# Shared expert's gate and up spread between the steps of the last batch's routing, its rows finished around the plan, and turnings late in the first round of expert tiles

## The chip, the cores and the metric

The kernel runs on one core of a Trainium2 chip. The metric is device time in microseconds (us) of one execution. Five engines run their own instruction streams and meet at semaphores: PE (TensorE, matmuls and transposes), DVE (VectorE), ACT (ScalarE), POOL (GpSimd, here almost only indirect DMAs) and SP (SyncE, plain DMAs).

## The reference, cut to what matters

One transformer layer in float32 on 4 batches of 512 tokens with 512 features: a modulated layer norm, linear attention, a second modulated layer norm, and a mixture of 64 experts with the best 8 per token, plus a shared expert that every token passes through.

```python
h = _layernorm(x) * (1 + cb) + sb                       # rows "h2"
logits = h @ gate_w.T                                   # 64 experts
topv, topi = top_k(logits, 8); rw = softmax(topv)
inter = silu(gate) * up                                 # per expert, 512 -> 128
out = einsum(inter * W[:, :, None], dp_w)               # 128 -> 512
sh_inter = silu(x @ sh_gate_w.T) * (x @ sh_up_w.T)      # shared expert
out = out + sigmoid(x @ sh_gate1_w.T) * (sh_inter @ sh_down_w.T)
x = x + gb * out
```

## The kernel before, in words

Everything is one unrolled program but for the loop over the experts' tiles. Attention and routing go batch by batch; `LAST` is batch 3. The order on each engine is the order in which the code is written, and each engine waits only at semaphores (`s_...`).

**Routing of the last batch** goes in two halves of two 128-token tiles each. For a half, PE turns the normalized rows (`turn_h2_half`), ACT copies them out of PSUM (`turned_h2_half`), PE scores them against the gate weights (`score_half`), DVE picks the best 8 (`choose_half`), PE ranks each pick within its expert (`rank`, two small bf16 matmuls per tile), and DVE works out the picks' slots (`places_half`). POOL writes each pick's token number to its slot in DRAM (`slot_table`) by an indirect DMA of 128 numbers (L587, 32 per batch). In the code, `landed` makes POOL wait after every 8 of them until they have landed.

**The plan** follows: PE counts each expert's tokens (`s_cnt`), DVE makes tiles of them (`s_ntile`), PE sums them up (`s_cum`), DVE compares (`s_past`), PE spreads that out (`s_flat`), DVE writes `plan` (`s_plan`, 2). Before the counting, DVE finishes the last batch's rows (`finish_h2`: 4 tiles, a multiplication and an addition each) and makes the routing weights (`weights`, ends with `s_wt`).

**SP** stores the finished rows when `s_h2` is complete and the routing weights when `s_wt` is; only behind these two in its order stand the loads of the first experts' weights (`load_w`) and of the slot table's parts (`load_table`), which alternate: weights 1, part 0, weights 2 and 3, part 1, and so on.

**Shared expert.** Batch 0's is done early. `KEPT` (batch 1), `HELD` (2) and `LAST` (3) come after the routing: `shared_gate_up` is 8 matmuls of 128x512 (4 for the gate, 4 for the up half; each shows as two rows of PE in the trace), ACT makes the silu (`shared_silu`), DVE the product (`shared_inter`), PE the product with the down weights (`shared_down`), DVE adds it to x (`shared_sum`). Between them stand DVE's first token lists (`first_tokens`: numbers 0 to 2 need part 0 of the table, 3 and 4 part 1), which release POOL's first gathers of rows (L634).

**The experts' tiles** go in rounds of 8, 20 rounds. Per tile of 128 tokens: PE turns the gathered rows (`turn`, L1710), gate and up (L1715), turning of the product (L1730), down (L1723); ACT and DVE work between. Round 0 is written out, the others loop. In the step of tile t, PE turns tile t+2 before the gate and up of tile t. ACT's order in a step is: copy of turned tile t+2 (`take_x`), weights of tile t (`own_pairs`), silu of tile t.

## Time and profile before

| | |
|---|---|
| median of 3 runs | 1062.57 us (1063.09, 1053.07, 1062.57) |
| profiled execution | 1062.77 us, span 1060.9 us |
| busy share of the span | PE 88%, PEld 54%, DVE 52%, ACT 25%, POOL 46% |
| mean granted TensorE clock | 0.956 of full |
| chain that ended last | PE 60%, "another core or an unknown queue" 10%, DVE 9%, issue 6%, DMA 5% |

The span runs from the first to the last instruction; 1.9 us of the execution lie outside it. The stretch that the change touches runs from about 304 us (last batch's rows turned) to about 410 us (end of round 0).

### The profile page before, as it was taken

The page shows a single profiled execution, that of the slowest core. Times are in us where ns is not written, and L with a number is a line of the kernel's source. Part 1 is how long each engine was busy: PE and PEld are TensorE (multiplying, and loading weights), DVE is VectorE, ACT ScalarE, POOL GpSimd, SP SyncE. Part 2 cuts the span into 40 slices and gives each one's busy share as a digit, 9 for nine tenths or more (in the row PEclk, how much of TensorE's full clock was granted, in tenths as well). Part 3 has the DMA queues.
Part 4 walks back from the last instruction along what each step waited for, and adds up shares of the span by engine and source line. Part 5 has one row for each costly group of instructions (what it writes and reads, how often), then busy time and mean ns, then how long its engine had stood idle before and what let it go on. Part 6 is the DMA issues. An engine that isn't in the chain of part 4 may idle for free.

```text
span 1060.9 us, 18619 instructions
## 1 busy us (share of the span) xinstructions
PE 929.2 (88%) x3569; PEld 570.0 (54%) x3570; DVE 546.4 (52%) x1457; ACT 261.8 (25%) x789; POOL 491.5 (46%) x480
## 2 busy tenths in 40 slices
PE   6999999999875789888989999888998899887697
PEld 2344444445342356666666666666666666655243
DVE  4777767885854333333433334333434334333888
ACT  2133132123120023322322223223332233222000
POOL 0500254264557355555555555555555555555500
PEclk9999999999987889999999999999999999999699
DMA  9940030030032326666656666666667665796697
GB/s 345 333 142 1 1 95 8 34 95 1 1 104 76 117 62 204 218 200 195 215 183 224 234 225 201 212 198 210 210 206 245 207 202 173 260 393 250 228 420 316
DMA packets 68519, 192.07 MB, mean 181 GB/s; under 512 B 19926, under 2 KB 20438, under 8 KB 68104
## 3 DMA queue, kind: packets, MB, share of 16 engines
q1 hardware_dynamic: 38232, 120.28, 32.3%
q0 software_dynamic: 30256, 71.43, 20.5%
q8 instruction: 12, 0.20, 0.1%
q14 instruction: 19, 0.16, 0.1%
HBM read 158.98 MB, written 52.54 MB: 199 GB/s over the span
## 4 chain that ended last, share of the span: by engine, by line
PE 60%; another core or an unknown queue 10%; DVE 9%; issue 6%; DMA 5%; DVEq 1%; ACTq 1%; ACT 1%; POOLq 0%; SPq 0%; POOL 0%
PE bank L1715 18%; PE bank L1723 12%; PE bank L1483 7%; PE bank L1710 6%; PE bank L1530 5%; PE bank L1784 3%; PE bank L1494 2%; PE bank L1730 2%; PE bank L1596 2%; DMA wqkv<-y_rows 1%; PE bank L1615 1%; DMA front<-y_rows 1%; DVE front L1328 1%; DMA y_rows<-front,sid 1%
## 5 line engine op out<-in xcount | busy, mean ns | idle before, releaser
L1715 PE MATMUL bank<-wqkv,h2T 128*128 x1280 | 313.2, 388 | 0.5 <-issue 0.5
L644 POOL DMA_INDIRECT y_rows<-front,sid x160 | 163.6, 1023 | 216.8 <-issue 82.4
L1715 PEld LDWEIGHTS bank<-wqkv,h2T 128*128 128x128 f32 x1280 | 238.1, 197 | 28.9 <-issue 1.6
L587 POOL DMA_INDIRECT slot_table<-pair,place x128 | 129.1, 1009 | 181.1 <-DVE place L1050 118.6
L634 POOL DMA_INDIRECT front<-h_rows,gid x167 | 170.9, 1023 | 74.4 <-issue 46.5
L1342 DVE COPY front<-bank 128x128 f32<-128x128 f32 x160 | 46.6, 291 | 271.8 <-remote 156.5
L1723 PE MATMUL bank<-wqkv,front 128*128 x320 | 173.7, 625 | 0.8 <-DVE front L1342 0.8
L830 ACT ACTIVATE h2T<-bank 128x512 f32<-128x512 f32 x162 | 96.5, 596 | 253.9 <-PE bank L1710 144.5
L1710 PEld LDWEIGHTS bank<-const,front 128*128 128x128 f32 x648 | 83.2, 146 | 100.4 <-issue 96.6
L1336 DVE COPY front<-bank 128x512 f32<-128x512 f32 x160 | 110.0, 688 | 45.1 <-PE bank L1723 34.1
L1483 PE MATMUL bank<-wqkv,front 128*128 128x512 f32 x256 | 113.8, 595 | 0.0
L1710 PE MATMUL bank<-const,front 128*128 128x128 f32 x648 | 102.5, 283 | 10.2 <-issue 5.5
L1730 PE MATMUL bank<-const,front 128*128 128x128 f32 x160 | 46.3, 290 | 58.7 <-DVE front L1328 55.3
L1483 PEld LDWEIGHTS bank<-wqkv,front 128*128 128x128 f32 x256 | 47.5, 190 | 56.3 <-issue 54.9
L1328 DVE SCALAR_TENSOR_TENSOR front<-bank,wgt,front 128x128 f32<-128x128 f32 x160 | 56.0, 350 | 29.9 <-ACT front L836 24.9
L836 ACT ACTIVATE front<-bank 128x128 f32<-128x128 f32 x160 | 43.4, 271 | 105.9 <-PE bank L1715 67.5
L1730 PEld LDWEIGHTS bank<-const,front 128*128 128x128 f32 x160 | 22.6, 141 | 78.6 <-DVE front L1328 57.8
L1494 PE MATMUL bank<-front,wqkv 128*128 128x512 f32 x128 | 59.3, 607 | 0.0
L1530 PE MATMUL bank<-front 128*128 128x512 f32 x128 | 56.6, 594 | 2.5 <-DVE front L1040 2.4
L1723 PEld LDWEIGHTS bank<-wqkv,front 128*128 128x128 f32 x320 | 49.1, 194 | 14.2 <-issue 3.4
L1784 PE MATMUL bank<-front,const 128*128 128x512 f32 x92 | 44.6, 635 | 8.5 <-DMA front<-y_rows 8.5
L845 ACT ACTIVATE wgt<-front 128x1 f32 x160 | 32.5, 203 | 72.4 <-issue 46.8
(254 smaller groups left out, 769.9 us busy)
## 6 DMA issues: line engine op xcount, KB each, us to landing
wqkv<-in_experts SPq DMA_DIRECT2D x64, 768.0 KB
front<-y_rows SPq DMA_DIRECT2D x20, 768.0 KB, 9.9
wqkv<-y_rows SPq DMA_DIRECT2D x12, 768.0 KB, 11.6
front<-in_w_mod SPq DMA_DIRECT2D x5, 1024.0 KB, 10.3
x<-in_x SPq DMA_DIRECT2D x4, 1024.0 KB, 11.1
h_rows<-h SPq DMA_DIRECT2D x4, 1024.0 KB
out_dram<-x SPq DMA_DIRECT2D x16, 256.0 KB, 8.4
wqkv<-in_w_in SPq DMA_DIRECT2D x3, 1024.0 KB, 13.5
```

The lines of the kernel that those rows point to most:

```text
L587: pool.indirect_dma_start(out=slots[:, :], out_offset=bass.IndirectOffsetOnAxis(ap=place[b % 2][:, i, k:k + 1], axis=0), in_=pair[:, b * T ...
L634: pool.indirect_dma_start(out=xg[s], out_offset=None, in_=h2_rows[:, :], in_offset=bass.IndirectOffsetOnAxis(ap=gid[:, s:s + 1], axis=0), ...
L644: pool.indirect_dma_start(out=y_rows[:, :], out_offset=bass.IndirectOffsetOnAxis(ap=sid[:, s:s + 1], axis=0), in_=yb[s % YBUFS], in_offset ...
L830: sc.activation(h2T[:, s % 4, :], bank[s % 2][:, :], ACT.Copy).then_inc(s_xT, 1)
L1336: ve.tensor_copy(yb[s % YBUFS], bank[4 + s % 2][:, :]).then_inc(s_y, 1)
L1483: mm = pe.matmul(bank[2 + j][:, :], hT[:, k, i * P:(i + 1) * P], win[:, k, (j + 1) * D:(j + 2) * D], start=(k == 0), stop=(k == KC - 1))
L1494: mm = pe.matmul(bank[4 + c % 2][:, :], win[:, k, c * P:(c + 1) * P], hT[:, k, :], start=(k == 0), stop=(k == KC - 1))
L1530: mm = pe.matmul(bank[4 + i % 2][:, :], qT[:, k, i * P:(i + 1) * P], woa[:, k, :], start=(k == 0), stop=(k == KC - 1))
L1710: mm = pe.transpose(bank[s % 2][:, k * P:(k + 1) * P], xg[s][:, k * P:(k + 1) * P], ident)
L1715: mm = pe.matmul(bank[2 + s % 2][:, 0:GU], xT[s % 4][:, k, :], wqkv[:, bass.ds(w + k * GU, GU)], start=(k == 0), stop=(k == KC - 1))
L1723: pe.matmul(bank[4 + s % 2][:, :], iT[s % 2], wqkv[:, bass.ds(w + KC * GU, D)], start=True, stop=True).then_inc(s_d, 1)
L1730: pe.transpose(bank[6 + s % 2][:, 0:P], inter[s % 2], ident).then_inc(s_I, 1)
```

## The change

Six edits, in three groups.

1. On PE, the gate and up of the shared expert, before a block behind the routing, are cut into pieces of 4 or 2 matmuls that stand between the steps of the last batch's routing (KEPT all, HELD's gate half) and of the plan (HELD's up half, LAST's both).
2. On DVE, `finish_h2` and `weights` of the last batch leave their place ahead of the counting. Two tiles are finished behind `s_ntile`, two behind `s_past`; `weights` stands behind the plan.
3. On POOL, `landed` is not called for batch 2. On PE, in round 0, the turning of tile t+2 stands behind tile t's gate and up, tile t-1's turning and tile t-2's down.

```diff
@@ POOL
                     scatter(b, n, n + TOPK)
-                    landed(b, n + TOPK)
+                    if b < LAST - 1:
+                        landed(b, n + TOPK)
@@ DVE, last batch
                         places_half(b, j, td)
-                    finish_h2(ve, b)
-                    weights(b)
                     ve.wait_ge(s_cnt, 1)
...
                     ve.tensor_copy(tiles_f[:, :], tiles_f[:, :]).then_inc(s_ntile, 1)
+                    finish_h2(ve, b, range(0, HT))
                     ve.wait_ge(s_cum, 1)
...
                     ve.tensor_scalar(past[:, :], const[0:EV, C_FLAT:C_FLAT + PLAN], cum[:, 0:1], None, ALU.is_ge).then_inc(s_past, 1)
+                    finish_h2(ve, b, range(HT, TPB))
                     shared_inner(KEPT)
...
                     ve.tensor_copy(plan[:, 1, :], plan_f[:, 1, :]).then_inc(s_plan, 1)
+                    weights(b)
                     ve.wait_ge(s_plan, 2)
                     first_tokens(range(0, 3))
@@ PE, shared_gate_up
-            def shared_gate_up(b, halves=range(2)):
+            def shared_gate_up(b, halves=range(2), chunks=range(KC)):
...
-                    for k in range(KC):
+                    for k in chunks:
...
-                if j == 1:
+                if j == 1 and k == KC - 1:
                     mm.then_inc(s_shg, 1)
@@ PE, last batch
                     turn_h2_half(b, 0)
+                    shared_gate_up(KEPT, range(0, 1))
                     score_half(b, 0)
+                    shared_gate_up(KEPT, range(1, 2), range(0, KC // 2))
                     turn_h2_half(b, 1)
                     rank(b, range(0, HT))
+                    shared_gate_up(KEPT, range(1, 2), range(KC // 2, KC))
                     score_half(b, 1)
+                    shared_gate_up(HELD, range(0, 1))
                     rank(b, range(HT, TPB))
@@ PE, plan
-            shared_gate_up(KEPT)
             pe.wait_ge(s_rd, BATCH)
             pe.matmul(bank[6][0:EV, 0:1], ...).then_inc(s_cnt, 1)
-            shared_gate_up(HELD, range(0, 1))
+            shared_gate_up(HELD, range(1, 2))
             pe.wait_ge(s_ntile, 1)
...
-            shared_gate_up(HELD, range(1, 2))
+            shared_gate_up(LAST, range(0, 1))
             pe.wait_ge(s_past, 1)
...
+            shared_gate_up(LAST, range(1, 2))
             shared_down(KEPT)
-            shared_gate_up(LAST)
             shared_down(HELD)
             shared_down(LAST)
@@ PE, a step of a round
-                    turn(t + 2, r + (s + 2) // ROUND, (s + 2) % ROUND)
+                    if again:
+                        turn(t + 2, r + (s + 2) // ROUND, (s + 2) % ROUND)
...
                         down(t - 2, (s - 2) % 2, w[s - 2])
+                    if not again:
+                        turn(t + 2, r + (s + 2) // ROUND, (s + 2) % ROUND)
```

In PE's order, from the second scoring of the last batch to the count, stood before (bank7 is the scoring, bank6 the rank and the count, bank2 and bank3 KEPT's gate and up):

```order
L1578 MATMUL bank7<-gate_w,xn 128x65 [waits s_arow,s_top,s_h2T]
L1578 MATMUL bank7<-gate_w,xn 128x65 x7
L1626 MATMUL bank6<-mask,tri_bf 128x65 [waits s_mask,s_rd,s_woa]
L1627 MATMUL bank6<-seen,ones_bf 128x65
L1626 MATMUL bank6<-mask,tri_bf 128x65 [waits s_mask]
L1627 MATMUL bank6<-seen,ones_bf 128x65
L1596 MATMUL bank2<-front,shared_w 128x512 [waits s_kvr,s_sht,s_again,s_shw]
L1596 MATMUL bank2<-front,shared_w 128x512 x3
L1596 MATMUL bank3<-front,shared_w 128x512 x4
L1689 MATMUL bank6<-ones_bf,seen 65x1 [waits s_rd]
```

and stands now, from the last piece of KEPT ahead of that scoring (bank4 is HELD's gate half):

```order
L1598 MATMUL bank3<-front,shared_w 128x512 [waits s_kvr,s_sht,s_again,s_shw]
L1598 MATMUL bank3<-front,shared_w 128x512
L1580 MATMUL bank7<-gate_w,xn 128x65 [waits s_arow,s_top,s_h2T]
L1580 MATMUL bank7<-gate_w,xn 128x65 x7
L1598 MATMUL bank4<-h2T,shared_w 128x512 [waits s_kvr,s_or,s_shw]
L1598 MATMUL bank4<-h2T,shared_w 128x512 x3
L1628 MATMUL bank6<-mask,tri_bf 128x65 [waits s_mask,s_rd,s_woa]
L1629 MATMUL bank6<-seen,ones_bf 128x65
L1628 MATMUL bank6<-mask,tri_bf 128x65 [waits s_mask]
L1629 MATMUL bank6<-seen,ones_bf 128x65
L1694 MATMUL bank6<-ones_bf,seen 65x1 [waits s_rd]
```

The count stood behind KEPT's 8 matmuls and stands now right behind the rank; HELD's gate half moved ahead of the rank.

In DVE's order, behind the last batch's places (`place1`), stood before:

```order
L1050 TENSOR_TENSOR place1<-spot_c,spot_p 128x16 [waits s_vd]
L391 TENSOR_TENSOR h2<-h2,rows_b 128x512 [waits s_tpC,s_rows_b]
L393 TENSOR_TENSOR h2<-h2,rows_b 128x512 [waits s_h2m]
...
L1080 SCALAR_TENSOR_TENSOR wtok,esum<-etop,mask 128x64 [waits s_ww,s_ex]
L1080 SCALAR_TENSOR_TENSOR wtok,esum<-etop,mask 128x64 x3
L1082 TENSOR_SCALAR sh1<-esh 128x4
L1083 RECIPROCAL gate_sh<-sh1 128x4 [waits s_vw]
L1084 RECIPROCAL rsum<-esum 128x4
L1085 TENSOR_TENSOR wtok<-wtok,rsum 128x256 [waits s_vw]
L1289 CAST count_i<-bank6 65x1 [waits s_cnt]
```

and between the plan and the first token stands now:

```order
L1311 CAST plan<-plan_f 1x200 [waits s_v]
L1312 CAST plan<-plan_f 1x200
L1081 SCALAR_TENSOR_TENSOR wtok,esum<-etop,mask 128x64 [waits s_ww,s_ex]
L1081 SCALAR_TENSOR_TENSOR wtok,esum<-etop,mask 128x64 x3
L1083 TENSOR_SCALAR sh1<-esh 128x4
L1084 RECIPROCAL gate_sh<-sh1 128x4 [waits s_vw]
L1085 RECIPROCAL rsum<-esum 128x4
L1086 TENSOR_TENSOR wtok<-wtok,rsum 128x256 [waits s_vw]
L1212 TENSOR_LOAD plan [waits s_tbl0,s_plan]
```

The weights, on which SP's store and with it all loads of the table wait, stood ahead of the count and stand now between the plan and the first token, which itself waits for part 0 of the table.

## Rows read from the trace of the kernel before

**Rows 1.** Stretches: length, then PE, PEld, DVE, ACT, POOL busy; clock, DMA share, GB/s

```profile
304.00:331.00 27.00, 11.66 (x60) 9.21 (x59) 11.83 (x56) 7.25 (x16) 18.30 (x20) 0.59 0.03 3
...
340.00:352.00 12.00, 1.70 (x6) 0.64 (x4) 1.26 (x9) 0.60 (x1) 7.15 (x8) 0.76 0.62 179
...
410.00:985.00 575.00, 511.01 (x2285) 366.94 (x2283) 216.56 (x612) 169.29 (x609) 314.56 (x309) 0.97 0.65 220
```

**Rows 2.** PE in order of time: start, us, line, tile, count [idle before <-releaser]

```profile
306.54 2.00 PE L1578 MATMUL bank<-gate_w,xn 128*128 128x65 f32 x16 [1.65 <-ACT xn L769]
...
316.85 3.68 PE L1578 MATMUL bank<-gate_w,xn 128*128 128x65 f32 x16 [1.44 <-issue]
...
328.90 8.98 PE L1596 MATMUL bank<-front,shared_w 128*128 128x512 f32 x16
...
337.75 3.68 PE L1596 MATMUL bank<-h2T,shared_w 128*128 128x512 f32 x8
...
352.34 5.79 PE L1596 MATMUL bank<-h2T,shared_w 128*128 128x512 f32 x8
...
362.37 7.03 PE L1596 MATMUL bank<-xn,shared_w 128*128 128x512 f32 x16
...
376.10 1.04 PE L1710 MATMUL bank<-const,front 128*128 128x128 f32 x8
...
379.46 1.95 PE L1715 MATMUL bank<-wqkv,h2T 128*128 x8
```

**Rows 3.** DVE in order of time, from a scoring's copy to the first token

```profile
312.90 0.29 DVE L1130 COPY logit<-bank 128x130 f32<-128x130 f32 x1 [3.20 <-remote]
...
326.48 0.29 DVE L1130 COPY logit<-bank 128x130 f32<-128x130 f32 x1 [6.49 <-remote]
...
331.11 0.69 DVE L391 TENSOR_TENSOR h<-h,rows_b 128x512 f32<-128x512 f32 x1
...
339.46 0.48 DVE L1085 TENSOR_TENSOR wtok<-wtok,rsum 128x256 f32<-128x256 f32 x1 [1.17 <-DVE rsum L1084]
350.12 0.15 DVE L1289 CAST count_i<-bank 65x1 int32<-65x1 f32 x1 [10.18 <-issue]
...
360.06 0.24 DVE L1311 CAST plan<-plan_f 1x200 int32<-1x200 f32 x1
361.34 0.15 DVE L1214 TENSOR_SCALAR gid<-tbl 128x1 int32 x1 [1.03 <-issue]
```

**Rows 4.** ACT in order of time, the silu of the kept batch

```profile
347.99 0.60 ACT L789 ACTIVATE shared_act<-bank 128x512 f32<-128x512 f32 x1 [16.32 <-remote]
```

**Rows 5.** POOL in order of time, scatters (L587) and gathers (L634)

```profile
300.61 0.96 POOL L587 DMA_INDIRECT slot_table<-pair,place  x1 [5.36 <-DMA slot_table<-pair,place]
...
331.47 1.16 POOL L587 DMA_INDIRECT slot_table<-pair,place  x1 [1.06 <-issue]
...
348.32 0.96 POOL L587 DMA_INDIRECT slot_table<-pair,place  x1 [0.30 <-remote]
362.49 1.04 POOL L634 DMA_INDIRECT front<-h_rows,gid  x1 [13.21 <-DVE gid L1214]
...
390.42 1.04 POOL L634 DMA_INDIRECT front<-h_rows,gid  x1 [6.30 <-DVE gid L1214]
```

**Rows 6.** SP in order of time, loads of the table's parts 0 and 1

```profile
341.20 0.34 SPq L488 DMA_DIRECT2D tbl<-slot_table  x1
...
350.47 0.33 SPq L488 DMA_DIRECT2D tbl<-slot_table  x1
```

**Rows 7.** DMA issues from 340 to 352 us, KB and us to landing

```profile
tbl<-slot_table SPq DMA_DIRECT2D x1, 16.0 KB, 3.9
```

**Rows 8.** PE in order of time, tile 7 of round 0 and the loop

```profile
407.74 1.89 PE L1715 MATMUL bank<-wqkv,h2T 128*128 x8
...
439.23 1.46 PE L1715 MATMUL bank<-wqkv,h2T 128*128 x6
```

**Rows 9.** DVE in order of time, in the loop

```profile
442.57 0.29 DVE L1342 COPY front<-bank 128x128 f32<-128x128 f32 x1 [5.62 <-remote]
```

## The prediction

> **What bounds the kernel now.** I read the page first, then the table of stretches, then each engine in order of time from 300 to 410 us. The loop of the experts' tiles, 410 to 985 us, is PE's: busy 511 of 575 us at a clock of 0.97 [rows 1]. The change leaves it and the end as they are, so what counts is when the loop gets going. Ahead of it, from 304 to 331 us, no engine is full: PE 11.7 of 27 us, at a mean clock of 0.59 [rows 1]. There the chain goes PE, ACT, PE, DVE and back, twice, for the routing, then through the plan. It ends in two things: the first gather, at 362.5 us [rows 5], and PE's first turning, at 376.1 us [rows 2], behind all of the shared expert. The first gather waited 13.2 us for DVE's token numbers, POOL having been free since 349.3 us [rows 5]; they followed the plan, done at 360.3 us [rows 3].
>
> One thing in this chain is no work. PE's rows end well before those who need them start. The second scoring is over at 320.5 us, DVE copies it at 326.48 [rows 2, 3]; KEPT's gate and up is over before HELD's begins at 337.75, ACT's silu of it starts at 347.99 [rows 2, 4]; DVE, ready at 339.94 us, gets the count only at 350.12 [rows 3]. I call this late results. It comes in the loop too: DVE idle 5.6 us until 442.57 while PE's rows go on [rows 8, 9]. I have no row that names the cause, and most of the uncertainty below is about what becomes of it.
>
> **The change, part by part.**
>
> *Count.* Before, DVE's places ended at 331.1 us, then came 8.8 us of finishing and weights (331.11 to 339.94), then 10.2 us of waiting [rows 3]. Now the count stands directly behind rank on PE and behind the places on DVE. Neither the 8.8 us nor KEPT's 8 matmuls (16 rows, 6.9 us at full clock, from 0.43 us a row) stand ahead of it. The wait of 10.2 us fell where DMA was busy for 0.62 of the time; from 304 to 331 us, where the count now goes, it was 0.03 [rows 1]. Bounds: 10.2 us of lateness again, or none. I take none, since a count this early meets neither that traffic nor that queue of gate and up. Count at 331.6 rather than 350.1: 18.5 us earlier.
>
> *Gate and up between the routing steps.* A piece of 4 matmuls is 3.4 us at full clock and double at half. The one ahead of the first scoring pushes it from 306.5 to 308.3, its end to 310.3; DVE used the result only at 312.90 [rows 2, 3], so lateness covers this; without that cover it costs 1.8 us. The next (2 matmuls, 1.7 us) lies beside ACT's norm. The one ahead of the second scoring could cost 1.7 us; against that the second scoring took 3.68 us where the first took 2.00 for the same 16 rows [rows 2], the clock having fallen to 1.2 GHz while PE idled; with PE fed it should take 2.0. These two cancel. HELD's gate half stands ahead of the last rank, but DVE has 2.2 us of choosing in between, and lateness ahead of that. Bounds for the whole: +5 (no cover) to -4. I take -1.3, giving a count at 330.3.
>
> *Count to plan.* Before: 350.12 to 360.3, 10.2 us, of which 5.8 us is a piece of HELD at mostly half clock [rows 2, 3]. Now this stretch has, on DVE in order: the count's steps 1.6, the sum 0.7, two tiles finished 2.7 (8 operations at 0.69 make four tiles 5.3 [rows 3]), the comparison 1.2, then PE's LAST piece and the spreading, 0.5 to 3, in whose shadow lie the other two tiles 2.7, the product 0.7 and the plan's own 1.4. Sum about 10.8. Plan at 341, 19 us earlier.
>
> *Weights and table.* This edit gives back. `weights` takes 3.5 us (the rest of the 8.8 after 5.3), so `s_wt` comes at 344.6: later than before (339.94) by 4.7 us. Queued behind it on SP: the store, then part 0 of the table, issued 1.3 us after the weights were done (341.20) and landing 3.9 us later [rows 3, 6, 7], then weights of experts 2 and 3, then part 1, issued 10.5 us after them (350.47) [rows 6]. Before, part 0 had landed long before the plan; now DVE waits for it: 344.6 + 5.2 = 349.8, first gather about 351. POOL is free by then, since it was at 349.3 with its last 14 scatters following places at 331.1 [rows 5], which now come 1.3 us earlier. First gather 11.5 us earlier.
>
> *POOL without waits for batch 2.* The longest of them was 5.4 us, at 300.6 [rows 5]. POOL then reaches the last batch's scatters earlier, but those wait for the places. Before, the second half's started right with its places, at 331.47 [rows 5], so the queue was no bound. Worth 0 in the likeliest case; if places come early (below), it lets the scatters follow.
>
> *PE's end of the shared expert.* Before, LAST's gate and up ran 362.4 to 369.2 and the down products to 376.1 [rows 2]. The 6.9 us are now done earlier, but what is late next is DVE: HELD's product stands behind tokens 0 to 2 (part 0), LAST's behind tokens 3 and 4 (part 1). Part 1 lands at 344.6 + 10.5 + 3.9 = 359; then the product 0.7, the down products 3.4 at full clock or up to 6.9 at half (PE has idled). First turning at about 365.5 instead of 376.1: 10.6 us earlier.
>
> *Round 0.* From first turning to tile 7's gate and up PE took 31.6 us (376.1 to 407.74 [rows 2, 8]) for 8 tiles; the loop needs 575 us for the other 152, 3.8 each with its own late results, 3.4 in busy time [rows 1]: 27 to 30 us. Waiting for gathers made part of the difference: gather 5 went out at 390.42, after POOL had waited 6.3 us for DVE [rows 5]. Turning late lets PE do gate and up of tile t while t+2 is still on its way. Its cost: `take_x` of t+2 stands ahead of tile t's silu on ACT, so that silu now follows the late turning instead of running in the shadow of gate and up; at most the 0.5 us of a turning a tile (two took 1.04 [rows 2]), 4 us in all. Bounds -5 to +4; I take -3, as the waits for gathers weigh more.
>
> **Sum:** -10.6 - 3 = -13.6 on the profiled execution's 1062.8 us, which is 0.2 over the median: **1049 us**. The fast one of the three runs before (1053.07) shows that some 10 us come and go by themselves.
>
> **Rivals.**
>
> *The late results go away.* Those of this stretch fall where PE mostly waits (11.7 of 27 us busy [rows 1]), and feeding it is what the pieces do. Then places come some 12 us earlier (4.4 ahead of the first copy, 6.0 ahead of the second [rows 2, 3], less at the rank). The scatters then bind: 20 of them at 1.26 us from about 316.8 end at 342. Plan 333, weights 336.5, part 0 at 341.7, first gather 343, part 1 at 351, first turning 357.5: 18.6 + 3 earlier, **1041**. Against: in the loop PE is fed and they occur [rows 8, 9].
>
> *The wait moves with the count.* If the 10.2 us of lateness meet the count wherever it is, the plan comes at 351, `s_wt` at 355, part 1 at 369, first turning at 376: only round 0 is left, **1060**. For it: DVE got both scoring results late as well, with no DMA traffic about.
>
> *The late results are PE's real pace.* KEPT's 16 rows then took 328.9 to 347.99, 1.2 us a row [rows 2, 4], not the 0.43 of the records. Now 24 such rows stand between the first turning of the last batch's rows and the count, against 16 before: 9.5 us later, and LAST's piece before the plan adds 3.7. Plan at 371 to 373, weights 3.5, part 1 at 390, first turning at 395 against 376.1; less round 0's 3: +16, **1079**. Between the likeliest case's -13.6 at 0.43 us a row and this +16 at 1.2 the break-even lies near 0.8. Against: the records do slow down with the granted clock (8.98 us for KEPT's 16 rows, 7.03 for LAST's, [rows 2]), so they follow the array. [...]
>
> **How the numbers follow.** Likeliest case 0.44, results on time 0.23, wait moved 0.24, real pace 0.09. What a measurement can tell from no change is about 1%, 10.6 us: faster means under 1052, slower over 1073. Faster: nearly all of the first (0.38) and second (0.22), 0.60. Slower: the last, 0.09. The rest 0.31. The range leaves out the last case and the tails of the others below 1036 and above 1063, together under 0.2.
>
> **What the profile of the changed kernel would show.** DVE's count within 2 us of the places' end (if 10 us later: wait moved). KEPT's pieces in PE's rows between 305 and 315, clock full there. SP's load of part 0 about 1.3 us behind DVE's weights, and DVE idle between them and the first token, which shows the new wait; first gather near 351; first turning near 365; in round 0 PE's gate and up with no gather ahead of them. The prediction is wrong if places move by more than 3 us either way, or if tile 7's gate and up is not some 13 us ahead of 407.7.

## The result and the profile after

The kernel after takes 1078.62 us (median of 4 runs, 1077.78 to 1079.36), the kernel before 1062.36 us beside it: a ratio of 1.0154, 95% interval 1.0111 to 1.0196. It is slower by 16 us, where 1049 us was forecast. All ratios here and below leave out single executions far above the rest of their kernel (three in all, of 1059.1, 1069.2 and 2416.1 us). The profiled execution took 1079.36 us, span 1077.5 us; PE was busy 87% at a clock of 0.953.

The stretches of [rows 1] after the change (same columns):

```profile
304.00:331.00 27.00, 16.74 (x50) 8.04 (x48) 11.89 (x41) 4.11 (x7) 7.68 (x8) 0.81 0.01 0
340.00:352.00 12.00, 9.59 (x31) 4.08 (x30) 7.43 (x31) 3.64 (x8) 8.95 (x11) 0.98 0.02 1
410.00:985.00 575.00, 513.63 (x2305) 368.77 (x2304) 217.45 (x618) 171.08 (x616) 315.69 (x309) 0.97 0.66 222
```

The loop is as it was. From 304 to 325 us PE is not at the routing at all, but still at the projection ahead of it, in code that the change does not touch. POOL of the kernel after, in order of time (its row of batch 2's 32 scatters begins and ends with the first two lines, the row of the last batch's 20 with the next two; then gathers 0 and 5):

```profile
272.77 0.96 POOL L587 DMA_INDIRECT slot_table<-pair,place  x1 [19.00 <-DVE place L1051]
...
313.01 0.96 POOL L587 DMA_INDIRECT slot_table<-pair,place  x1 [0.30 <-issue]
336.50 0.96 POOL L587 DMA_INDIRECT slot_table<-pair,place  x1 [22.53 <-DVE place L1051]
...
360.71 0.96 POOL L587 DMA_INDIRECT slot_table<-pair,place  x1 [0.30 <-issue]
375.39 1.04 POOL L635 DMA_INDIRECT front<-h_rows,gid  x1 [13.72 <-DVE gid L1215]
...
403.11 1.05 POOL L635 DMA_INDIRECT front<-h_rows,gid  x1 [6.08 <-DVE gid L1215]
```

DVE of the kernel after in order of time, which answers to [rows 3]: the additions of the last projection (L1099), the two scoring copies, the count, the sum, the plan, the end of the weights, tokens 0 and 3:

```profile
306.38 0.69 DVE L1099 TENSOR_TENSOR x<-bank,x 128x512 f32<-128x512 f32 x1 [13.49 <-issue]
...
318.31 0.69 DVE L1099 TENSOR_TENSOR x<-bank,x 128x512 f32<-128x512 f32 x1 [9.39 <-remote]
...
331.48 0.29 DVE L1131 COPY logit<-bank 128x130 f32<-128x130 f32 x1 [0.47 <-PE bank L1580]
...
337.71 0.29 DVE L1131 COPY logit<-bank 128x130 f32<-128x130 f32 x1 [1.49 <-PE bank L1580]
...
343.38 0.15 DVE L1288 CAST count_i<-bank 65x1 int32<-65x1 f32 x1
...
350.13 0.15 DVE L1299 COPY cum<-bank 65x1 f32<-65x1 f32 x1 [2.52 <-issue]
...
364.93 0.35 DVE L1308 TENSOR_TENSOR plan_f<-bank,const 1x200 f32<-1x200 f32 x1 [10.37 <-remote]
...
367.27 0.42 DVE L1086 TENSOR_TENSOR wtok<-wtok,rsum 128x256 f32<-128x256 f32 x1
374.24 0.15 DVE L1215 TENSOR_SCALAR gid<-tbl 128x1 int32 x1 [6.54 <-issue]
...
384.38 0.15 DVE L1215 TENSOR_SCALAR gid<-tbl 128x1 int32 x1 [4.89 <-issue]
```

PE of the kernel after: the turning of the last batch's rows, the product for the plan, the first turning and tile 0's gate and up, tile 7's:

```profile
325.17 1.04 PE L1569 MATMUL bank<-const,h 128*128 128x128 f32 x8
...
351.85 0.88 PE L1703 MATMUL bank<-past,ones 65*1 65x200 f32 x2
...
391.02 1.04 PE L1715 MATMUL bank<-const,front 128*128 128x128 f32 x8
392.55 1.99 PE L1720 MATMUL bank<-wqkv,h2T 128*128 x8 [0.49 <-issue]
...
427.25 3.27 PE L1720 MATMUL bank<-wqkv,h2T 128*128 x8
```

Read together: DVE waits 13.5 and 9.4 us for the projection's results (0.8 and 0.9 us before the change) while POOL issues scatters without a break, and the turning of the last rows comes at 325 instead of about 304 us. The first turning is 14.9 us later than before (376.10 in [rows 2]); most of the loss is there. Between, all went much as designed: no late copies, the count right behind the places, at a clock of 0.98. Then POOL's next row begins at 336.5, and the plan's numbers, whose PE rows end at 352.7, reach DVE at 364.9. That is 3 us behind the end of POOL's row; the addition at 318.31 came 4 us behind the end of the row ahead of it.

### The profile page after: what moved, and what is told of

It is laid out like the page before. It is cut to its first block, busy times and chain, and to the rows that moved or that the text cites. A ratio compares the mean times of both kernels' runs of the same rounds, so it can differ in the third digit from the quotient of the medians.

```text
span 1077.5 us, 18621 instructions
## 1 busy us (share of the span) xinstructions
PE 932.7 (87%) x3569; PEld 568.0 (53%) x3570; DVE 546.0 (51%) x1457; ACT 261.8 (24%) x789; POOL 490.6 (46%) x480
## 4 chain that ended last, share of the span: by engine, by line
PE 62%; another core or an unknown queue 10%; DVE 8%; issue 7%; DMA 3%; ACTq 1%; DVEq 1%; ACT 1%; SPq 0%; POOLq 0%
PE bank L1720 20%; PE bank L1728 12%; PE bank L1485 7%; PE bank L1715 6%; PE bank L1532 4%; PE bank L1792 4%; PE bank L1735 2%; PE bank L1496 2%; DMA front<-y_rows 2%; PE bank L1598 1%; DVE front L1330 1%; PE bank L1558 1%; DVEq L1212 1%; ACTq L841 1%
## 5 line engine op out<-in xcount | busy, mean ns | idle before, releaser
L587 POOL DMA_INDIRECT slot_table<-pair,place x128 | 128.2, 1001 | 194.6 <-DVE place L1051 142.4
L1344 DVE COPY front<-bank 128x128 f32<-128x128 f32 x160 | 46.7, 292 | 269.9 <-remote 164.8
L1532 PE MATMUL bank<-front 128*128 128x512 f32 x128 | 61.9, 636 | 18.8 <-DVEq L1100 8.2
L1532 PEld LDWEIGHTS bank<-front 128*128 128x128 f32 x128 | 25.4, 204 | 51.5 <-issue 34.3
## 6 DMA issues: line engine op xcount, KB each, us to landing
wqkv<-y_rows SPq DMA_DIRECT2D x12, 768.0 KB, 10.4
wqkv<-in_w_in SPq DMA_DIRECT2D x3, 1024.0 KB, 13.5
```

The costliest lines, as they stand in the source:

```text
L587: pool.indirect_dma_start(out=slots[:, :], out_offset=bass.IndirectOffsetOnAxis(ap=place[b % 2][:, i, k:k + 1], axis=0), in_=pair[:, b * T ...
L1532: mm = pe.matmul(bank[4 + i % 2][:, :], qT[:, k, i * P:(i + 1) * P], woa[:, k, :], start=(k == 0), stop=(k == KC - 1))
```

## The experiments

They ran in several groups of runs. The kernel before itself took 1062.4 us beside the result, 1044.8, 1048.4, 1046.6 and 1046.6 us beside experiments 1 to 4, 5 to 8, 9 to 12 and 13 to 15, and 953.4 us beside 16 to 18, so each ratio is to the kernel before of the same group. Each group of experiments also ran on another chip (numbers 8, 9, 15, 0 and 13 in this order), so where ratios of different groups are held against each other, the chip differs too. Brackets are 95% intervals; times inside a kernel are read from one profiled execution each.

**1. POOL's waits back** in the kernel after.

```diff
-                    if b < LAST - 1:
-                        landed(b, n + TOPK)
+                    landed(b, n + TOPK)
```

> The changed kernel with POOL's waits after every 8 scatters of batch 2 put back; all else as changed. Theory A (POOL's unbroken row of scatters makes PE's results late): the last projection is used on time again, its first addition on DVE near 293.5 us instead of 306.4 and the turning of the last batch's rows near 304 instead of 325; the time falls by 15 to 25 us, to 1054 to 1064. Theory B (the late results belong to PE's new order or to the place of its code): the first addition stays near 306, the time within 3 us of 1078.6.

Ratio 1.0045 [0.9992, 1.0099]. The turning of the last rows is back at 303.77 us and the count at 332.3. The plan was late by itself: DVE waited 9.3 us for it, until 350.2, 0.6 us after POOL's last pick (349.63) began.

**2. The POOL edit alone** on the kernel before (the diff of 1 the other way round).

> The kernel before with nothing but POOL's edit: no waits for landing in batch 2. Theory A: the last projection's first addition moves from 293.9 to about 306 us and the rows' turning from 304 to about 325; what was late behind it before (23 us from 307 to 350) is partly spared, since POOL has a pause then; time 1062 to 1080. Theory B: the same time as before, 1062, with the turning at 304.

Ratio 1.0074 [1.0030, 1.0118]: +7.7 us for the edit that I had held at nothing. Two of DVE's additions of the projection waited 4.5 and 10.8 us for PE, first scoring 320.2 us; POOL's row ended at 314.3:

```profile
318.20 0.69 DVE L1099 TENSOR_TENSOR x<-bank,x 128x512 f32<-128x512 f32 x1 [10.81 <-remote]
```

**3. As 1, turnings early again** in round 0.

> As e1_landed_back, and the turnings of round 0 early again, as before the change. If late turnings cost up to 0.5 us a tile without cover: 3 to 4 us faster than e1_landed_back. If they spare waits for gathers, as forecast: 3 us slower than it. If neither: within 2 us of it.

Ratio 0.9960 [0.9911, 1.0008], not clear of no change. Only the reordering is left: count 334.5, plan done 344.4, first gather 353.9, first turning 370.3, tile 7 at 404.0 us.

**4. A wait behind every scatter** of batch 2, in the kernel after.

```diff
-                for n in range(0, TOPK * TPB, TOPK):
+                step = 1 if b == LAST - 1 else TOPK
+                for n in range(0, TOPK * TPB, step):
```

> The changed kernel with POOL waiting after every single scatter of batch 2. The 32 scatters then take some 32 x 2.4 = 77 us instead of 41 and end near 350 us, so the scatters of the last batch and the first gather come 10 to 15 us later than they would. Theory A: the projection is on time (first addition near 293.5), PE's results from 289 to 340 are never over 2 us late. Theory B: late as in the changed kernel. Time by A 1060 to 1075, by B over 1085.

Ratio 1.0343 [1.0299, 1.0387]. No result was late from 285 to 335 us (all waits of DVE for PE at most 1.5 us) and the rank was read at 320.3 us. A scatter with its wait took 2.42 instead of 1.27 us, POOL came to its first gather at 386.2, and that is the loss.

**5. Turnings late alone**, on the kernel before.

```diff
-                    turn(t + 2, r + (s + 2) // ROUND, (s + 2) % ROUND)
+                    if again:
+                        turn(t + 2, r + (s + 2) // ROUND, (s + 2) % ROUND)
...
+                    if not again:
+                        turn(t + 2, r + (s + 2) // ROUND, (s + 2) % ROUND)
```

> The kernel before with one edit alone: in round 0 the turning of tile t+2 stands behind the down products instead of ahead of gate and up. The forecast held this at -3 us with bounds -5 to +4 (ratio near 0.997). The two runs that differ from each other in this edit (with the POOL waits back and the turnings late, and the same with the turnings early) differ by 7.5 us, and if the edit acts alone, the time here is the kernel before's plus 7 us, ratio near 1.007, with tiles 3 to 7 of round 0 at 3.5 us each or more, where with early turnings they follow at 3.1. If those 7.5 us came from an interplay with the other edits, this run is within 2 us of the kernel before.

Ratio 1.0062 [1.0033, 1.0091], +6.5 us. PE, gate and up of tiles 3 to 7 in this run, and DVE's gating behind ACT's silu:

```profile
389.56 1.89 PE L1715 MATMUL bank<-wqkv,h2T 128*128 x8
...
393.01 1.89 PE L1715 MATMUL bank<-wqkv,h2T 128*128 x8
...
396.58 1.89 PE L1715 MATMUL bank<-wqkv,h2T 128*128 x8
...
400.14 1.89 PE L1715 MATMUL bank<-wqkv,h2T 128*128 x8
...
408.90 2.60 PE L1715 MATMUL bank<-wqkv,h2T 128*128 x8
```

```profile
391.12 0.35 DVE L1328 SCALAR_TENSOR_TENSOR front<-bank,wgt,front 128x128 f32<-128x128 f32 x1 [2.35 <-ACT front L836]
```

3.5 us a tile, where experiment 3 has 3.14 (384.01 to 396.56 us for 4 tiles): silu follows the late turning's copy on ACT. Most of the loss is elsewhere. From the first turning to tile 2's gate and up it is 12.5 us here and 14.1 before, from there to tile 6 14.1 and 13.7; then tile 7 comes 8.8 us behind tile 6 instead of 3.8. ACT took tile 7's turned rows some 4 us after PE's rows had ended in both kernels, but only with late turnings did PE stand still for it. ACT's copy and PE's next turning of a product, here and then in the kernel before:

```profile
404.56 0.60 ACT L830 ACTIVATE h2T<-bank 128x512 f32<-128x512 f32 x1 [6.51 <-remote]
...
406.32 0.33 PE L1730 MATMUL bank<-const,front 128*128 128x128 f32 x1 [4.28 <-DVE front L1328]
```

```profile
404.01 0.60 ACT L830 ACTIVATE h2T<-bank 128x512 f32<-128x512 f32 x1 [3.44 <-remote]
...
406.15 0.33 PE L1730 MATMUL bank<-const,front 128*128 128x128 f32 x1 [0.30 <-DVE front L1328]
```

From first turning to tile 7 it is 35.4 us here, 31.6 before [rows 2, 8]. So about 4 of the 6.5 us are seen here, one late result's worth, in two traces of different groups; the rest I did not trace. Experiments 1 and 3 differ by 8.9 us, but there 6.7 us stood ahead of the first turning, from a plan that happened to be late in 1 and not in 3, and from first turning to tile 7 they differ by only 0.5 us (34.1 and 33.7).

**6. Batch 1's scatters in one row** in the kernel before.

```diff
+                    if b != 1:
                         landed(b, n + TOPK)
```

> The kernel before with the waits behind each 8 scatters dropped for batch 1 instead of batch 2: POOL's 32 scatters of that batch run in one row from 204.5 to about 245 us. No result of PE comes late there with the waits (204 to 254 us). Theory A (it is the length of POOL's unbroken row of indirect DMAs that delays PE's signals): results of PE come late from some 16 scatters on, 225 to 245 us, by up to 10 us, and batch 2's projection and routing with them; the run is slower than the kernel before by 5 to 15 us. Rival B (it is how many scatters have been issued in all, late ones only from about the 70th): nothing comes late before 289 us, and POOL's row ends some 8 us earlier at no other change; time within 3 us of before.

1072.2 us (one run), 24 us over the kernel before. POOL's last scatter of the row, and DVE's next use of a PE result (with the waits in place that addition came at 225.4):

```profile
246.91 0.96 POOL L587 DMA_INDIRECT slot_table<-pair,place  x1 [0.30 <-issue]
```

```profile
250.72 0.69 DVE L1099 TENSOR_TENSOR x<-bank,x 128x512 f32<-128x512 f32 x1 [24.41 <-remote]
```

Rival B, the count of all scatters, falls: this is 62 us before the first late result of the kernel before (312.90 [rows 3]).

**7. POOL waits for the projection**, in the kernel after.

```diff
+                    elif b == LAST - 1 and n == 0:
+                        pool.wait_ge(s_mv2, LAST + 2)
```

> The kernel after with one wait added: behind the first 8 scatters of batch 2 POOL waits until DVE has used the last projection (s_mv2), and then issues the other 24 in one row from about 310 to 340 us. Theory A (late results go with a row of scatters at that very time): the last batch's projection is back on time, DVE's adds at 294, 297, 302, 305 us and PE's turning at 304 as in the kernel before, and then the routing results within the row come late: copies of logit and rank 4 to 12 us after PE's rows end, count near 343, plan after 360; the time stays near that of the kernel after, as POOL's picks of the last batch start only at 340. Rival C (the last projection was late in the kernel after for another reason, such as PE's or DVE's own order): it is late here too, turning at 325.

1076.8 us (one run). The projection is on time (turning at 306.0), so rival C falls. POOL's row now lasts from 311.4 to 367.3 us, and DVE waits 10.1 and 25.9 us for PE's rank and sum; the sum's PE rows were over at 341.2:

```profile
340.93 0.27 PE L1700 MATMUL bank<-const,tiles_f 65*1 65x65 f32 x2
```

```profile
366.35 0.96 POOL L587 DMA_INDIRECT slot_table<-pair,place  x1 [0.30 <-issue]
```

```profile
334.08 0.29 DVE L1154 CAST rank_i<-bank 128x128 int32<-128x128 f32 x1 [10.09 <-remote]
...
368.39 0.16 DVE L1301 COPY cum<-bank 65x1 f32<-65x1 f32 x1 [25.90 <-issue]
```

Late results follow the row wherever it is put.

**8. Weights ahead of the plan**, in the kernel of 3 (`weights(b)` behind `s_past`).

> The kernel after with batch 2's POOL waits back, round 0's turnings early again, and the weights put behind the comparison that gives past, ahead of the plan, instead of behind the plan. With the weights behind the plan they ended at 345.8 us, the table's part 0 left at 346.9, POOL's row ended at 353.0, the first gather went at 353.9, the first turning at 370.3, tile 7's gate and up at 404.0. Now the weights should end near 341.5, part 0 leave near 342.6 and land near 348, so that the first gather is POOL's bound alone: 353.3, no more than 0.6 us earlier, and part 1 of the table, behind two loads of weights, lands near 359 instead of 363.5, so that LAST's product and down products end and the first turning comes at 366 instead of 370.3. If this reaches the loop, tile 7 comes near 400 and the time is 4 us under that of the same kernel with weights late (ratio to before 0.992); if round 0 is bound by POOL's picks and gathers, the gain is spent there and the ratio stays at 0.996.

Ratio 0.9967 [0.9937, 0.9997], as in 3. The first gather did not gain (354.7 us): the weights ended at 341.8, but SP's store of the finished rows stands ahead of theirs, and half of these rows were now finished behind the weights, at 344.4; part 0 left at 346.7, as in 3. The first turning came at 368.6, and the second waited 5.8 us; tile 7 at 402.7.

**9. The kernel of 3 without the pieces** between the routing steps.

> The kernel with POOL's waits back and the turnings early, whose count was right behind the places (334.5 us) and whose ratio to before was 0.996; here PE's gate and up pieces are taken out from between the routing steps again and stand behind the count (all of KEPT there, HELD's halves behind the sums and behind the comparison, LAST behind KEPT's down products, as before). What is left of the change is that count, plan and half of the finishing go ahead. My forecast held the pieces at -1.3 us net for the routing (-4 to +5), and they take 6.9 us of LAST's gate and up off the end. By that: count within 2 us of 333, plan at 343 or 2 to 4 us later since KEPT stands whole ahead of the sums, first turning not earlier than with the pieces, and a time some 2 to 5 us above the version with them, ratio 0.998 to 1.001. Rival: the pieces bring nothing, since PE waits for the table anyway, and the ratio is 0.996 again.

Ratio 1.0022 [1.0003, 1.0041], 0.6% above 3, with intervals that just overlap. The count came at 328.3 us, 6.2 us earlier than with the pieces, but the sum was 14.1 us late (346.7), in POOL's row from 323 to 349 us. Since 3 had no such wait, the 0.6% is not shown to be the pieces' own worth.

**10 and 11. Shorter rows for batch 2**, in the kernel of 8: the last 16 scatters in pairs, and the first 6 picks too (10), or those 16 in fours and nothing else (11).

```diff
+                    step = 4 if b == LAST - 1 and n >= 2 * TOPK else TOPK
+                    for m in range(n, n + TOPK, step):
+                        scatter(b, m, m + step)
+                        landed(b, m + step)
```

> The version with POOL's waits back, turnings early and weights ahead of the plan (count 332 us, first gather 354.7), with POOL pausing more often where PE's results are needed: the last 16 scatters of batch 2 and the first 6 of the last batch in pairs, a wait for the landing behind each. Theory A (rows of indirect DMAs delay PE's signals, a pause lets them through; single scatters with a wait each had none late): no copy or rank of DVE waits over 2.5 us between 300 and 325 us, places at 317 and 322, count near 323 instead of 332, 9 us earlier. POOL pays: a pair costs 3.7 us instead of 2.5, so batch 2 ends near 325, the first 6 picks near 336, the other 14 near 354 as before, so that the first gather stays at 354 and the time within 2 us of the same version without pairs (ratio 0.997). Rival: if 8 us of lateness stay although POOL pauses every 3.7 us, it is not the length of the rows.

> The same version with the last 16 scatters of batch 2 in fours and the picks in one row. POOL pays about 2 x 1.2 us more for batch 2 (end near 324 us) and nothing for the picks. Theory A with a delay that grows with the row: the copy of the first scoring is late by under 2 us (3.9 in rows of 8) and the rank by under 4 (7.8), count near 325 to 328, POOL's row of 20 picks from about 326 to 350, first gather at 352 or 1 to 3 us earlier than without, ratio 0.992 to 0.997. If the length of a row does not matter below 8, count is at 332 again and the ratio 0.998.

10: ratio 1.0067 [1.0046, 1.0088]; 11: 0.9967 [0.9939, 0.9994]. In both no wait for a routing result was over 1.5 us, the count came at 322.5 and 323.5 us, and the plan was done at 333.7 and 334.9, 10 us earlier than in 3. The time didn't follow. In 10 POOL's own pauses cost it: the first gather went at 364.9 us, 11 us later than in 3. In 11, PE (the turnings of tiles 0 and 1, the next one, gate and up of tile 0), ACT's first use of them, and POOL's last of 37 DMAs in a row:

```profile
364.71 1.04 PE L1716 MATMUL bank<-const,front 128*128 128x128 f32 x8
378.32 1.09 PE L1716 MATMUL bank<-const,front 128*128 128x128 f32 x4 [12.57 <-issue]
379.20 2.81 PE L1721 MATMUL bank<-wqkv,h2T 128*128 x8
```

```profile
377.58 0.60 ACT L832 ACTIVATE h2T<-bank 128x512 f32<-128x512 f32 x1 [43.03 <-issue]
```

```profile
373.06 0.96 POOL L587 DMA_INDIRECT slot_table<-pair,place  x1 [0.30 <-issue]
```

What was won ahead of the plan in 11 was lost to the next late result, 12 us at the start of round 0.

**12. The kernel after again.**

> The kernel after, unchanged, on the chip of the experiments, so that the edits can be held against it on one scale. The parts measured here: POOL's waits away alone +7.7 us on the kernel before, late turnings alone +6.5 us, everything else -4.2 us (turnings early, waits back). If they add up, ratio 1.010; if the missing waits cost more where count and plan stand close behind the routing, as the first trace of the kernel after shows (turning of the last rows 21 us late, where it was 5 us late with the waits away alone), 1.015 to 1.022.

Ratio 1.0094 [1.0068, 1.0120]. The parts add up within their intervals: reordering -0.4%, POOL edit +0.7%, turnings +0.6%, together +0.9%. (Its chip is that of 9 to 11; 1 to 8 ran on two others.) In this group of runs the turning of the last rows came at 317.5 us, not 325.2, and the first turning at 382.5, not 391.0; the 6 us by which the result's 1.0154 is worse go with 8 us more lateness of the same kind.

**13. Pauses in round 0's first picks too**, in the kernel of 11.

```diff
-            scatter_picks(2, range(TPB))
+            for j, k in enumerate(PICKS[2]):
+                for n in range(TPB):
+                    put_pair(LAST, n, k, s_scat_last[2])
+                pool.wait_ge(s_scat_last[2], 16 * TPB * (j + 1))
```

> The version with fours in batch 2 (plan at 333 us, first gather 352.4, first turning 364.7, but ACT takes that turning only at 377.6, 3.6 us behind the end of POOL's row of 37 indirect DMAs at 374.0), with two more pauses: the 8 picks behind the first three gathers in two fours, each followed by a wait for its landing. Theory A: the turning of tile 0 is taken within 3 us (368 or earlier) or behind the next pause of POOL (about 362 and 368 to 369), so gate and up of tile 0 starts near 370 instead of 379.2, gather 5 goes near 376 instead of 384.2, and tile 7's gate and up starts near 396 instead of 404.8: 8 us faster than without, ratio to before 0.987 to 0.991. Rival D: round 0 is bound by something else, such as the table's later parts or the weights, and the ratio stays at 0.997 with tile 7 at 404 or later.

Ratio 0.9938 [0.9908, 0.9968], the best of its group, though the gain over 11 is less than forecast and the intervals overlap. ACT took the turning at 368.8 instead of 377.6, behind the pause near 367, though PE's rows had ended near 362; tile 7 came at 399.5 instead of 404.8.

**14. Fours alone**, on the kernel before.

> The kernel before with one edit: the last 16 scatters of batch 2 in fours with a wait for the landing behind each, instead of in eights. Theory A: the two scoring results and the ranks reach DVE on time, as they did with this edit in the changed kernel (places at 316 and 323 instead of 325 and 331), so everything up to the count's PE rows is 8 us earlier; the count's result then meets POOL's unbroken row of picks (14 to 20 scatters from 326 to 351) and stays late, 345 to 352, so that of 8 us only 0 to 5 reach the plan: ratio 0.995 to 1.000. If the ratio is under 0.993, late results in the routing alone were worth more than the whole reordering.

Ratio 1.0064 [1.0041, 1.0087]. The plan was ready for DVE at 337.5, 21 us earlier than before with nothing reordered, and gather 0 went at 351.3; but LAST's gate and up, a result within POOL's next row (325.7 to 373.0 us), reached ACT only 30 us after PE's rows had ended. PE, then ACT:

```profile
340.97 7.03 PE L1598 MATMUL bank<-xn,shared_w 128*128 128x512 f32 x16
```

```profile
377.84 0.60 ACT L791 ACTIVATE front<-bank 128x512 f32<-128x512 f32 x1 [40.48 <-remote]
```

**15. Empty instructions instead of waits**, in the kernel after: 30 behind every 4 scatters of batch 2.

> The kernel after, with 30 empty instructions on POOL behind every 4 scatters of batch 2, and no wait for a landing. If they take over 1 us together, POOL issues in fours with a gap. Theory A1 (a gap in the issuing is what lets PE's results through): the last projection is on time, turning of the last rows at 304 to 306 us instead of 317 to 325, and count near 322 to 325; ratio to before 1.000 to 1.005 (turnings late still cost their 6.5). Theory A2 (the DMAs must have landed, so that a gap without waiting does nothing): turning of the last rows at 315 or later and the ratio stays at 1.009 to 1.015. If the gaps come out under 0.5 us each, the run says nothing.

Ratio 1.0103 [1.0043, 1.0164], but the scatters kept their 0.30 us gaps, so nothing follows.

**16 to 18**, in a last group of runs: the kernel after with four small index fills on POOL behind every 4 scatters of batch 2 (16), the kernel before with the pauses of 11 and 13 (17), the kernel of 13 with those 8 picks in pairs (18).

```diff
+                            for i in range(4):
+                                pool.iota(idle[:, :], pattern=[[1, 32]], base=0, channel_multiplier=0).then_inc(s_fill, 1)
+                                pool.wait_ge(s_fill, m + i + 4)
```

> The kernel after; in batch 2 POOL does four small index fills, each waited for, behind every 4 scatters, and waits for no landing. If they take over 1 us together, POOL's row has gaps of that size (the landing waits made gaps of 1.5 us). Theory A1 (a gap in issuing suffices): the last projection on time, turning of the last rows near 304 to 306 us (317 without), count near 325, ratio 1.000 to 1.005. Theory A2 (it takes landed DMAs): turning at 315 or later, ratio 1.009 or more, since POOL ends batch 2 some 10 us later too.

> The kernel before with pauses alone: the last 16 scatters of batch 2 in fours, and the 8 picks behind the first gathers in fours, a wait for the landing behind each; nothing is reordered. With the first of the two alone the plan came at 337.5 us and gather 0 at 352, but ACT's silu of LAST only at 377.8, so that first turning was 384.4 and the ratio 1.0064. Theory A: the pauses near 361 and 368 let LAST's gate through, silu near 362 to 369, first turning 368 to 376, ratio 0.992 to 1.000. If silu stays near 377, the pauses are too short or come at the wrong time, and the ratio is 1.006 again.

> The reordered version with fours in batch 2 (ratio 0.9967) or with fours there and in the 8 picks behind the first gathers (0.9938, ACT took tile 0's turning at 368.8 though PE turned it at 361.1, and its silu was 4.2 us late); here those 8 picks go in pairs. Theory A: turning 0 is taken near 363 to 365, gate and up of tile 0 starts near 366, tile 7 near 395 instead of 399.5, at 3 us more for POOL, whose gather 3 goes at 371 instead of 368: ratio 0.990 to 0.993. Rival: gather 3 and the table's later parts, now later, set round 0, and the ratio is 0.994 or above.

Ratios 1.0017 [1.0002, 1.0031], 1.0049 [1.0033, 1.0064] and 1.0090 [1.0075, 1.0104]. The question of 16, pause or landing, could not be answered, since in the traces of this group nothing was late, in the loop neither. The costliest waits of DVE (us in total, times, longest), in the kernel after and in 17:

```profile
DVE front L1344 <- remote: 164.8, 36, 6.3
DVE front L1344 <- PE bank L1735: 67.7, 47, 3.0
```

```profile
DVE front L1347 <- PE bank L1735: 174.0, 158, 6.5
```

The 164.8 us of late results ("remote") are gone, and the kernel before takes 953 us here instead of 1045 to 1062. POOL's rows are the same: in 16, 39 DMAs from 324.1 to 373.8 us without a pause, and amid them PE goes from the first turning straight to tile 0:

```profile
360.91 1.04 PE L1722 MATMUL bank<-const,front 128*128 128x128 f32 x8
362.44 1.99 PE L1727 MATMUL bank<-wqkv,h2T 128*128 x8 [0.49 <-issue]
...
390.28 1.89 PE L1727 MATMUL bank<-wqkv,h2T 128*128 x8
```

So the rows do harm only together with something that this group of runs, or its chip, lacked. Pauses then only cost. The change costs little here either: 16 holds all of it, with fills that slow POOL besides, and is at 1.0017. Nor does it gain much: first turning 360.9 us in 16, 362.8 in 17, where nothing is reordered. What the reordering takes off in the other groups is then mostly what late results cost there; that is read from two traces and not tested by itself.

## Why the prediction was wrong

- *POOL without waits for batch 2*, "Worth 0 in the likeliest case", is the step that failed. I asked only whether POOL's queue was a bound. The rows held one hint, had I laid POOL's beside the late results of [rows 3, 4]: the count reached DVE at 350.12, 1 us behind the end of POOL's row of scatters (its last began at 348.32 [rows 5]). I had "no row that names the cause". Shown: +0.7% alone (2), and late results that follow the row (4, 6, 7). The ratio with the waits put back, 1.0045 against 1.0094 (1 and 12), points the same way, but the two are of different groups and their intervals overlap.
- *Round 0*, "I take -3": the sign was wrong, +6.5 us in the time (5). Both named effects are seen and are small: up to tile 2 late turnings gain 1.7 us, and the named cost, ACT's copy ahead of silu, is 0.4 us a tile. The term left out is the slack: with late turnings PE stood still 4.3 us for a late copy that cost it 0.3 us before (5).
- *Count*, "Bounds: 10.2 us of lateness again, or none. I take none": right in the kernel after (343.38, no wait), and as far as the trace goes for a reason that I didn't have, POOL pausing from 314 to 336 us.
- *Gate and up between routing steps*, -1.3 with bounds +5 and -4: against 9 the count comes 6.2 us later with the pieces, and the whole is still 0.6% faster; both differences hold late results, so what the pieces are worth stays open. Where none was late (10), the count with pieces came at 322.5 us.
- *Count to plan*, 10.8 us: 9.9 in experiment 3 (334.5 to 344.4), where nothing was late. In the kernel after 22.9, by the 10.4 us of lateness for the plan, which I had not allowed for there.
- *Weights and table*: the new wait is there (6.5 us at 374.24, after weights that ended at 367.7), forecast 5.2 us. The weights take 1.5 us, not 3.5: of the 8.8 us of [rows 3] 2 were waits. Part 1 reached DVE 16.7 us after the weights, 14.4 forecast.
- *PE's end*, -10.6 us: the reordering alone (3) gave -5.8 at the first turning, -3.8 at tile 7 and -0.4% of the time. From the count (-15.6) to the first gather (-8.6) it lost to POOL's 20 scatters, which end at 353.0 us there, then to part 1. Experiments 11 and 14 show that an even earlier plan is worth as little while results are held up in POOL's rows behind it.

Against the forecast's sum of -13.6 us stand, in the groups of the experiments, +7.7 for POOL's edit (2), +6.5 for the turnings (5) and -4.2 for the reordering (3), together +10 us, which is what 12 has; the result's +16 holds more lateness still.

The third rival named 1079 us and the measurement 1078.6, but by another road. Its mechanism, a PE that is really slower than its records, does not hold: in 4, 10 and 11 the same rows are used within 1.5 us. The Trainium skill (TensorE: Matmul & The Clock Gate, Seeing it yourself) warns that single clock events of a trace should not be fully trusted; nothing in the rows here needs a wrong clock for an explanation. That the number fits is luck.

What stays open is what makes the late results possible: why POOL's rows hold up PE's results in five groups of runs and not in the sixth. Chip and time changed together between the groups, so neither can be named. Whether a gap in POOL's issuing lets the results through or only a landing is open too.

## What to carry to other kernels

Before you remove a wait as useless, lay that engine's row beside the waits of all others: a long unbroken row of indirect DMAs on POOL went with PE results up to 30 us late, and a wait of 1.5 us every 4 DMAs ended that for the routing's results (11, 14). An earlier step is worth only what the next shared thing lets through; check each later hand-over (here table, POOL's row, start of round 0) before you sum. Measure such a change at more than one time and on more than one chip: the late results, and with them some 90 us of this kernel's time, were there in five groups of runs and gone in the sixth.

## What the runs showed of the hardware

- PE's completed rows can be used by DVE and ACT much later than they end, up to 30 us (14), while POOL issues indirect DMAs 1.27 us apart. The engines' waits grow with the row: for routing results at most 2.7 us in fours (14; as long in 17, where nothing was late), 3.9 and 7.8 in eights (8), 9 to 26 in rows of 20 and more (1, 6, 7, 9). Most of the long ones ended within 5 us of the row's end, some inside it (334.08 in 7). Not every result in a long row is late: the plan was in 1 and not in 3, whose programs are the same up to there.
- The effect was absent in one group of runs, on one chip, where the kernel before took 953.4 us, and there POOL's rows were as long.
- 30 empty instructions on POOL between two scatters left their gap at 0.30 us; four small index fills with waits made it 1.4 us.
